# Two-layer gated cross-attention and MoE kernel: layer 0's row return and layer 1's preparation in one block, scales for eight tiles at once, rows normalised on ScalarE

## The chip, the cores and the metric

One core of one Trainium2 chip runs the kernel. The metric is the device time of one execution in microseconds (us). A difference of 0.2% is about what a measurement of this kernel can tell from none.

## What is computed

Two layers over x (2048 rows of 256, fp32). Each layer is a gated cross-attention and a gated mixture of experts, both on a layer norm without parameters. The context has 1601 rows of 192, 16 heads of 16.

```python
x = x + tanh(g_xattn[0]) * L0_xattn(_layernorm(x), ctx_768, ...)
x = x + tanh(g_ffn[0]) * L0_ffn(_layernorm(x), ...)      # shared expert + top 1 of 8
x = x + tanh(g_xattn[1]) * L1_xattn(_layernorm(x), ctx_768, ...)   # with an MLP behind it
x = x + tanh(g_ffn[1]) * L1_ffn(_layernorm(x), ...)      # top 2 of 8, norm with gamma, beta

def _layernorm(x, axis=-1, eps=1e-05):
    m = jnp.mean(x, axis=axis, keepdims=True)
    v = jnp.var(x, axis=axis, keepdims=True)
    return (x - m) / jnp.sqrt(v + eps)
```

In the attention, q is projected from the normed x, k and v from the context; the scores are exponentiated without subtracting a maximum, unless a bound on them is exceeded.

## The kernel before

x stays in SBUF as 16 tiles (128 rows by 256 columns each); four tiles make a block of 512 rows (TB is 4, NB is 4). `ps` is PSUM, 8 banks of 512 fp32. A layer runs as a sequence of `nc.Block`s; at the end of a block all engines meet. In a block each engine has its own list of instructions, in the order written, and waits on semaphores.

1. **Preparation** (L507). `transpose_block` (L634) turns four tiles of xn on TensorE into banks 0 and 1, ScalarE copies them (`turned`, L574), TensorE projects them with wq (`item`, eight matmuls, L652), ScalarE takes squares and the bf16 high part (L591, L592), VectorE splits off the middle and low parts (L736, L741, L743), SyncE stores the parts (L354). Layer 0 has four items of keys before the four of queries; layer 1 only those of queries, since its keys were made in layer 0. `norm` (L346) sums squares by head. At the end the largest norms give `unsafe` (L767 to L775). In layer 0 `norm_rows` makes xn here for eight tiles at once.
2. **The check block** (L798). If `unsafe` is set, all scores are scanned for maxima first; otherwise it is skipped.
3. **Attention** (L928). Four blocks of queries, each with 104 exponentials on ScalarE (L1182), fed by TensorE (L948, L964). Behind it come routing and loads; layer 0 also makes layer 1's keys here.
4. **Experts** (L1603). For each of 23 tiles (39 in layer 1) GpSimd fetches 128 rows (L1842), TensorE transposes (L1639) and multiplies (L1652, L1664), GpSimd scatters the result (L1855). In layer 0, TensorE and ScalarE then make layer 1's values (L375, L381). SyncE waits for the last scatter, reads the rows back in four pieces (L1612), spreads the ones row of the keys and loads layer 1's first keys (L361). VectorE, for each piece of four tiles, adds the rows to x (L1814) and calls `norm_rows`: statistics (L457), `norm_root` (L438 to L450, a chain in which each small instruction waits for the one before), and xn (L461).
5. `free_semaphores` (L290) clears the layer's semaphores, with a meeting of all engines.

Then layer 1's preparation starts; its first instructions on SyncE are seven loads of weights (w1, b1, w2, the two halves of b2, rw, rb; L544 to L553). `norm_scales` (L471) is used at the end of layer 1: it writes a scale and a shift for each row, and ScalarE (L1737) applies them.

Of the kernel before, what the change touches and what calls it, by code (L numbers as in the profile page):

```python
# [20 lines left out]
ALU = mybir.AluOpType  # L21
# [61 lines left out]
def build(nc, a, out):  # L83
    ctx = ExitStack()
    with ctx:
# [203 lines left out]

        def free_semaphores():  # L290
# [31 lines left out]
        s_wk, s_wv, s_wq, s_kin = ([keep(f"{w}_in{l}") for l in range(2)] for w in ("wk", "wv", "wq", "k2"))  # L322
# [89 lines left out]
        def consts_pool(pool):  # L412
# [20 lines left out]
                           allow_small_or_imprecise_dtypes=True)  # L433

# [39 lines left out]
        def layer(L):  # L474
            l = L.n
            NTL, T = L.tiles, L.slots

            s_w, s_xn, s_rs, s_m1p = sem(f"attn_weights{l}"), sem(f"xn{l}"), sem(f"rest{l}"), sem(f"mid_parts{l}")
            s_xt, s_xtc = sem(f"xn_transposed{l}"), sem(f"xnT_copied{l}")
            s_pr, s_hi, s_sp = sem(f"projected{l}"), sem(f"high_parts{l}"), sem(f"split{l}")  # L480
            s_po = [sem(f"parts_stored{l}_{i}") for i in range(PARTS)]
            s_v, s_va, s_vz = sem(f"v_projected{l}"), sem(f"v_copied{l}"), sem(f"v_padded{l}")
            s_sq, s_nrm = sem(f"squared{l}"), sem(f"norm_sums{l}")
            s_top, s_turn = sem(f"norm_top{l}"), sem(f"norm_turned{l}")
            s_k2, s_q2 = [sem(f"k2_in{l}_{g}") for g in range(NG)], [sem(f"q2_in{l}_{g}") for g in range(NG)]
            s_ctx = [sem(f"ctx_in{l}_{i}") for i in range(2)]
            s_rw = sem(f"router_in{l}")
# [19 lines left out]
            with nc.Block() as block:  # L507
                @block.sync
                def _(sp):
                    def store(n):  # L510
                        kind, b = items[n]
                        w = width(n)
                        sp.wait_ge(s_sp, n + 1)
                        store_parts(sp, (k_img if kind == "k" else q_img)[l],
                                    [part[n % PARTS][j][:, :, 0:w] for j in range(3)],
                                    slice(b * w, (b + 1) * w), kind == "q", s_po[n % PARTS])

                    if l == 0:
                        src = a["x"].rearrange("o (p t) d -> p (o t) d", p=P)

                        def load_x(b):
                            sp.dma_start(x[:, b * TB:(b + 1) * TB, :], src[:, b * TB:(b + 1) * TB, :]).then_inc(s_x[b], 16)

                        load_x(0)
                        load_x(1)
                        load_wk(sp, 0)
                        for i, cols in enumerate([slice(0, 2 * KB), slice(2 * KB, M)]):
                            for k in range(2):
                                sp.dma_start(ctxT[0:CH, k, cols], a["ctxT"][k * CH:(k + 1) * CH, cols]
                                             ).then_inc(s_ctx[i], 16)  # L530
                        load_wv(sp, 0)
                        load_x(2)
                        load_x(3)
                        load_wq(sp, 0)
                        for i, name in enumerate(["g_xattn", "g_ffn"]):
                            sp.dma_start(gates[:, 2 * i:2 * i + 2], spread(a[name], 2)).then_inc(s_gate, 16)
                        sp.wait_ge(s_zero, 1)
                        for i in range(2):
                            sp.dma_start(shift_dram[i].rearrange("r h s -> (r h) s").rearrange("a (n s) -> a n s", n=4),
                                         zero[0:SHIFT * H, 0:D].bitcast(BF16).unsqueeze(1)  # L540
                                         .broadcast_to([SHIFT * H, 4, 2 * D])).then_inc(s_sz, 16)
                        spread_ones(sp, s_k2[0])
                    if L.mlp:
                        sp.dma_start(w1[:, :, :], a["w1"].rearrange("(k p) n -> p k n", p=P)).then_inc(s_w, 16)  # L544
                        sp.dma_start(b1[:, :], a["b1"]).then_inc(s_w, 16)
                        sp.dma_start(w2[:, :, :], a["w2"].rearrange("(k p) n -> p k n", p=P)).then_inc(s_w, 16)
                    else:
                        sp.dma_start(w2[:, 0:KD, :], a["wo"].rearrange("(k p) n -> p k n", p=P)).then_inc(s_w, 16)
                    for i in range(2):
                        sp.dma_start(b2[:, i, :], spread(a[f"bo{l}"], D)).then_inc(s_w, 16)  # L550
                    sp.dma_start(rw[:, :, :], a[f"rw{l}"].rearrange("(k p) n -> p k n", p=P)).then_inc(s_rw, 16)
                    if l == 1:
                        sp.dma_start(rb[:, :], spread(a["rb1"], E)).then_inc(s_rw, 16)  # L553

                    for n in range(Q0):
                        store(n)
# [1356 lines left out]
```

## Time and profile before

| | |
|---|---|
| median of 3 runs | 1501.73 us (1501.42 to 1502.45) |
| the profiled execution | 1500.18 us, span 1498.4 us |
| TensorE busy | 1351.1 us, 90% |
| ScalarE busy | 975.1 us, 65% |
| VectorE busy | 549.3 us, 37% |
| GpSimd busy | 175.6 us, 12% |
| mean granted TensorE clock | 0.951 of full speed |

The profile names an instruction by line, engine, operation and tiles. PE is TensorE, ACT ScalarE, DVE VectorE, POOL GpSimd, SPq the queue of SyncE. The chain that ended last goes back through the expert loop of layer 1 (L1652 and L1664, 5% and 4% of the span) and doesn't reach the stretch between the layers; it has to be read by its timeline.

### The profile page before, as it was taken

What the parts mean: (1) busy time and instruction counts of PE and PEld (TensorE: products, weight loads), DVE (VectorE), ACT (ScalarE), POOL (GpSimd) and SP (SyncE); (2) the same over time, 40 slices, a digit from 0 to 9 for tenths busy, and PEclk for the clock granted to TensorE, in tenths of its full rate; (3) what the DMA queues carried; (4) which work ended last, traced back from release to release, by engine and by line L of the source; (5) the groups of instructions that cost most, each with busy time, mean ns of one, the idle gap of its engine ahead of it and who ended that gap; (6) DMA issues with size and microseconds to landing.
All of it is one profiled execution on the core that took longest, in us unless ns stands there. A gap on an engine that the chain in (4) does not pass through costs nothing. (4 is left out here: it accounts for less than half of the span.)

```text
span 1498.4 us, 31951 instructions
## 1 busy us (share of the span) xinstructions
PE 1351.1 (90%) x13236; PEld 716.5 (48%) x13236; DVE 549.3 (37%) x1242; ACT 975.1 (65%) x1162; POOL 175.6 (12%) x188
## 2 busy tenths in 40 slices
PE   7799999999999996999657999999999994399994
PEld 4433333333333654999533334334334333299983
DVE  7412152242423253443550222422422524544435
ACT  4499999999996323333137996995996990055532
POOL 2000000000001321333200000000000000166530
PEclk9899999999999997999878999999999997599997
DMA  7661010101011714111439110110111115012214
GB/s 209 157 119 27 20 26 20 27 20 26 23 33 60 247 56 142 40 47 47 109 93 179 26 27 15 34 27 16 33 27 46 65 33 166 18 58 75 72 59 166
DMA packets 65866, 100.82 MB, mean 67 GB/s; under 512 B 10074, under 2 KB 47966, under 8 KB 64952
## 3 DMA queue, kind: packets, MB, share of 16 engines
q1 hardware_dynamic: 59768, 82.47, 20.2%
q0 software_dynamic: 5952, 16.26, 3.3%
q8 instruction: 108, 1.77, 0.5%
q14 instruction: 38, 0.31, 0.1%
HBM read 67.99 MB, written 26.21 MB: 63 GB/s over the span
## 5 line engine op out<-in xcount | busy, mean ns | idle before, releaser
L1182 ACT ACTIVATE arena<-ps 128x1024 f32<-128x1024 f32 x556 | 553.9, 1219 | 57.2 <-PE ps L948 57.2
L948 PE MATMUL ps<-arena 99*32 99x512 bf16 x6656 | 465.9, 384 | 15.4 <-PEq L798 9.4
L948 PEld LDWEIGHTS ps<-arena 99*32 99x32 bf16 x6656 | 151.3, 95 | 405.8 <-issue 167.0
L1182 ACT ACTIVATE wqkv<-ps 128x1024 f32<-128x1024 f32 x276 | 294.3, 1221 | 22.7 <-PE ps L948 22.7
L964 PE MATMUL ps<-arena 128*32 128x512 f32 x2224 | 290.5, 594 | 1.0 <-ACT arena L1182 0.8
L1264 DVE COPY work<-ps 128x512 f32<-128x512 f32 x32 | 22.1, 692 | 405.4 <-PE ps L964 405.4
L1652 PEld LDWEIGHTS ps<-work,arena 128*128 128x128 f32 x1184 | 144.6, 195 | 6.5 <-DVE work L1745 3.5
L1652 PE MATMUL ps<-work,arena 128*128 128x128 f32 x1184 | 145.7, 279 | 2.1 <-DVE work L1745 2.1
L964 PE MATMUL ps<-wqkv,arena 128*32 128x512 f32 x1104 | 144.0, 593 | 0.0
L1842 POOL DMA_INDIRECT work<-xn_img,fetch x62 | 60.9, 983 | 628.7 <-POOLq L928 612.8
L1664 PE MATMUL ps<-arena,work 128*128 x496 | 117.2, 380 | 0.0
L1268 DVE RECIPROCAL work<-work 128x512 f32<-128x512 f32 x32 | 107.3, 3353 | 1.1
L964 PEld LDWEIGHTS ps<-arena 128*32 128x32 f32 x2224 | 68.8, 111 | 59.6 <-ACT arena L1182 2.6
L1664 PEld LDWEIGHTS ps<-arena,work 128*128 128x128 f32 x496 | 89.4, 190 | 10.1 <-issue 0.5
L1706 ACT ACTIVATE arena<-arena 128x1024 f32 x62 | 65.3, 1057 | 32.2 <-PEq L928 23.4
L1855 POOL DMA_INDIRECT y_tok<-work,dest x62 | 61.8, 996 | 141.4 <-DVE work L1780 81.3
L1579 POOL TENSOR_TENSOR arena<-arena 128x512 f32<-128x512 f32 x12 | 17.5, 1460 | 490.5 <-ACT arena L1202 490.5
L1723 ACT ACTIVATE work<-work 128x512 f32<-128x512 f32 x39 | 24.6, 630 | 74.2 <-DVE work L1760 74.2
L1717 ACT ACTIVATE work<-ps 128x512 f32<-128x512 f32 x23 | 13.7, 597 | 90.6 <-PE ps L1652 90.6
L1745 DVE COPY work<-ps 128x256 f32<-128x256 f32 x62 | 26.3, 425 | 119.1 <-PE ps L1639 119.1
L1290 DVE TENSOR_TENSOR work<-ps,b 128x512 f32<-128x512 f32 x16 | 11.1, 692 | 109.9 <-PE ps L989 104.6
L964 PEld LDWEIGHTS ps<-wqkv,arena 128*32 128x32 f32 x1104 | 34.2, 111 | 29.0 <-ACT wqkv L1182 0.7
(204 smaller groups left out, 1157.7 us busy)
## 6 DMA issues: line engine op xcount, KB each, us to landing
arena<-in_ew SPq DMA_DIRECT2D x16, 512.0 KB, 5.3
arena<-q_img SPq DMA_DIRECT2D x32, 192.0 KB
arena<-y_tok SPq DMA_DIRECT2D x12, 512.0 KB, 6.3
arena<-k_img SPq DMA_DIRECT2D x8, 624.0 KB, 12.9
q_img<-work SPq DMA_DIRECT2D x18, 256.0 KB, 2.6
k_img<-work SPq DMA_DIRECT2D x21, 208.0 KB, 2.5
arena<-q_img SPq DMA_DIRECT2D x32, 128.0 KB
work<-work SPq DMA_DIRECT2D x128, 32.0 KB, 2.0
```

Of the source, the lines that this page charges most:

```text
L948: last = nc.tensor.matmul(ps[i * VW:(i + 1) * VW, buf + j, :], k2[0:ROWS + SHIFT, h, at:at + VW], q2[0:ROWS + SHIFT, h, :], start=True, st ...
L964: last = nc.tensor.matmul(ps[j * VW:(j + 1) * VW, 6 + g % 2, :], v_aug[:, c, HG * g + j, :], probs[(b * STEPS + 2 * w + j // 2) % RING][:, ...
L1182: nc.scalar.activation(probs[(b * STEPS + u) % RING], ps[:, buf:buf + 2, :], ACT.Exp, scale=SCALE).then_inc(s_exp, 1)
L1264: nc.vector.tensor_copy(pv_sb, ps[:, 6 + g % 2, :]).then_inc(s_copy, 1)
L1268: nc.vector.reciprocal(sums, sums).then_inc(s_inv, 1)
L1652: last = nc.tensor.matmul(ps[:, 2 + 2 * (i % 2) + n, f * P:(f + 1) * P], w_now[i % 2][n][:, k, f * P:(f + 1) * P], rowsT[i % 2][:, k, :], ...
L1664: last = nc.tensor.matmul(ps[:, 6 + i % 2, 0:D], hT[i % 2][:, k, :], w_down[:, bass.ds(e, 1), k, :].rearrange("p a n -> p (a n)"), start=( ...
L1706: nc.scalar.activation(w_now[i % 2][0].rearrange("p k n -> p (k n)"), w_gate[l][:, bass.ds(e, 1), :, :].rearrange("p a k n -> p (a k n)"), ...
L1723: nc.scalar.activation(hT[i % 2], act_g[i % 2], ACT.Relu).then_inc(s_h, 1)
L1745: nc.vector.tensor_copy(rowsT[i % 2], ps[:, i % 2, 0:D].rearrange("p (k n) -> p k n", n=P)).then_inc(s_tc, 1)
L1842: nc.gpsimd.indirect_dma_start(out=rows_in[i % ROWBUFS], out_offset=None, in_=xn_img[l], in_offset=bass.IndirectOffsetOnAxis(ap=fetch[:, i ...
L1855: nc.gpsimd.indirect_dma_start(out=y_tok[l], out_offset=bass.IndirectOffsetOnAxis(ap=dest[:, i:i + 1], axis=0), in_=rows_out[i % 2], in_of ...
```

## The change

- The preparation becomes a function `prepare(l)` that returns the parts of each engine. Layer 0's stays a block of its own. Layer 1's is appended to layer 0's expert block, so that the engines don't meet between the row return and it. Its semaphores are kept over the end of the layer, and `free_semaphores` now runs behind it.
- Layer 1's seven loads of weights are issued by SyncE at the start of layer 0's expert block.
- VectorE adds two pieces of rows, takes statistics for eight tiles, and calls `norm_scales` once for the eight; this is done twice, for both halves.
- xn is written by ScalarE: eight activations (Identity with a scale and a bias for each row) for each half, the first half before `turned(0)`, the second behind item 0. TensorE's transposes of block b wait for 4(b + 1) of them.
- In layer 1's preparation TensorE does item 1 before the transposes of block 2, and blocks 2 and 3 before item 2.
- At layer 0's start the padding of the values shares the constants' counter on GpSimd. Semaphores that only one layer needs are made once.

```diff
@@ layer 0's expert block
                 @block.sync
                 def _(sp):
                     if l == 0:
+                        preps[1][0](sp)
                         sp.wait_ge(s_dn, NTL)
...
                     if l == 0:
-                        spread_ones(sp, s_kin[1], 2)
+                        spread_ones(sp, s_kin, 2)
                         for i in range(2):
                             sp.wait_ge(s_kd[i], 96)
-                        load_k2(sp, 1, 0, s_kin[1])
+                        load_k2(sp, 1, 0, s_kin)
+                        preps[1][1](sp)
...
                             project_v(c, c % 4).then_inc(s_v, 1)
+                        pe.wait_ge(s_va, NC)
+                        pe.wait_ge(s_y, NTL)
+                        preps[1][3](pe)
...
                             copy_v(c, c % 4).then_inc(s_va, 1)
+                        preps[1][2](act)
...
                     if l == 0:
-                        for b in range(NB):
-                            ts = slice(b * TB, (b + 1) * TB)
-                            dve.wait_ge(s_back[b], 16)
-                            chain(nc.vector.scalar_tensor_tensor(
-                                out=x[:, ts, :].rearrange("p t d -> p (t d)"),
-                                in0=got[0][:, ts, :].rearrange("p t d -> p (t d)"), scalar=tg,
-                                in1=x[:, ts, :].rearrange("p t d -> p (t d)"), op0=ALU.mult, op1=ALU.add))
-                            chain(norm_rows(chain, lambda t: x[:, b * TB + t, :], lambda t: xn[:, b * TB + t, :]))
+                        n = 2 * TB
+                        for i in range(2):
+                            for b in range(2 * i, 2 * i + 2):
+                                ts = slice(b * TB, (b + 1) * TB)
+                                dve.wait_ge(s_back[b], 16)
+                                last = nc.vector.scalar_tensor_tensor(
+                                    out=x[:, ts, :].rearrange("p t d -> p (t d)"),
+                                    in0=got[0][:, ts, :].rearrange("p t d -> p (t d)"), scalar=tg,
+                                    in1=x[:, ts, :].rearrange("p t d -> p (t d)"), op0=ALU.mult, op1=ALU.add)
+                            chain(last)
+                            for t in range(n):
+                                last = nc.vector.bn_stats(stats[:, t, :], x[:, i * n + t, :])
+                            norm_scales(chain, last, n, scales[:, 0, i * n:(i + 1) * n],
+                                        scales[:, 1, i * n:(i + 1) * n]).then_inc(s_lnx, 1)
+                        preps[1][4](dve, chain)
@@ prepare(l), layer 1's parts
+                def normed(i):
+                    act.wait_ge(s_lnx, i + 1)
+                    for t in range(i * 2 * TB, (i + 1) * 2 * TB):
+                        nc.scalar.activation(xn[:, t, :], x[:, t, :], ACT.Identity, bias=scales[:, 1, t:t + 1],
+                                             scale=scales[:, 0, t:t + 1]).then_inc(s_nx, 1)
...
+                else:
+                    normed(0)
+                    turned(0)
+                    turned(1)
+                    act.wait_ge(s_wq[l], 48)
+                    item(0)
+                    normed(1)
+                    turned(2)
+                    item(1)
+                    turned(3)
+                    item(2)
+                    item(3)
...
+                def transpose_block(b):
                     if l == 0:
+                        pe.wait_ge(s_xn, b // 2 + 1)
+                    else:
+                        pe.wait_ge(s_nx, TB * (b + 1))
...
+                else:
+                    transpose_block(0)
+                    transpose_block(1)
+                    pe.wait_ge(s_wq[1], 48)
+                    item(0)
+                    item(1)
+                    norm(0)
+                    transpose_block(2)
+                    transpose_block(3)
+                    item(2)
+                    norm(1)
+                    item(3)
+                    norm(2)
+                    norm(3)
@@ consts and padding
-                        consts_pool(pool)
-                        pad_v(Chain(pool, "v_pad_chain"))
+                    pad_v(consts_pool(pool))
```

## Rows read from the trace of the kernel before

**Rows 1.** Windows: stretch, length, busy us (instructions) per engine, clock, DMA share, GB/s.
```profile
735.00:759.00 24.00, 0.00 (x0) 0.00 (x0) 21.89 (x96) 0.33 (x1) 0.00 (x0) 0.55 0.41 66
```
**Rows 2.** Timeline, VectorE, layer 0's row return: start, us, instruction, count [idle before].
```profile
732.19 1.28 DVE L1814 SCALAR_TENSOR_TENSOR x<-arena,tgate,x 128x1024 f32<-128x1024 f32 x1 [8.09 <-DMA arena<-y_tok]
...
733.51 1.40 DVE L457 BATCH_NORM_STATS2 stats<-x 128x6 f32<-128x256 f32 x4
...
737.82 1.38 DVE L461 TENSOR_SCALAR xn<-x,mv,root_bits 128x256 f32<-128x256 f32 x4
...
758.94 1.38 DVE L461 TENSOR_SCALAR xn<-x,mv,root_bits 128x256 f32<-128x256 f32 x4
```
**Rows 3.** Timeline, layer 1's preparation from its first transpose to the flag.
```profile
762.11 1.94 PE L634 MATMUL ps<-ident,xn 128*128 128x128 f32 x8 [27.20 <-PEq L293]
...
767.17 1.02 ACT L574 ACTIVATE arena<-ps 128x1024 f32<-128x1024 f32 x1 [2.06 <-PE ps L634]
...
771.72 0.68 ACT L592 ACTIVATE work<-ps,bq 128x512 bf16<-128x512 f32 x1
...
784.50 0.68 ACT L592 ACTIVATE work<-ps,bq 128x512 bf16<-128x512 f32 x1
...
785.29 1.41 DVE L736 SCALAR_TENSOR_TENSOR work<-ps,bq,work 128x512 f32<-128x512 f32 x2
...
791.08 0.14 DVE L775 TENSOR_SCALAR unsafe<-tops 1x1 int32<-1x1 f32 x1
```
**Rows 4.** Timeline, flag and first exponential: layer 0's two, then layer 1's exponential.
```profile
61.75 0.14 DVE L775 TENSOR_SCALAR unsafe<-tops 1x1 int32<-1x1 f32 x1
...
68.63 3.77 ACT L1182 ACTIVATE arena<-ps 128x1024 f32<-128x1024 f32 x4 [7.82 <-PE ps L948]
...
797.11 3.77 ACT L1182 ACTIVATE arena<-ps 128x1024 f32<-128x1024 f32 x4 [2.61 <-PE ps L948]
```
**Rows 5.** DMA issues of the second and fourth row read (us to landing); window, TensorE only.
```profile
arena<-y_tok SPq DMA_DIRECT2D x1, 512.0 KB, 4.8
...
arena<-y_tok SPq DMA_DIRECT2D x1, 512.0 KB, 8.7
...
730.00:735.00 5.00, 4.91 (x23) 1.00 0.98 368
```
**Rows 6.** Timeline, layer 0's preparation: statistics and xn of its second eight tiles.
```profile
31.24 2.71 DVE L457 BATCH_NORM_STATS2 stats<-x 128x6 f32<-128x256 f32 x8
...
37.16 2.67 DVE L461 TENSOR_SCALAR xn<-x,mv,root_bits 128x256 f32<-128x256 f32 x8
```
**Rows 7.** Timeline, end of layer 1: scales written by VectorE, applied by ScalarE.
```profile
1477.42 0.17 DVE L470 COPY scales<-root_bits 128x8 f32<-128x8 f32 x1
...
1477.70 3.76 ACT L1737 ACTIVATE arena<-ps,scales 128x256 f32<-128x256 f32 x8 [24.86 <-DVE scales L471]
```
**Rows 8.** Page, part 5: groups of ScalarE from SBUF and from PSUM (mean ns).
```profile
L1723 ACT ACTIVATE work<-work 128x512 f32<-128x512 f32 x39 | 24.6, 630 | 74.2 <-DVE work L1760 74.2
L1717 ACT ACTIVATE work<-ps 128x512 f32<-128x512 f32 x23 | 13.7, 597 | 90.6 <-PE ps L1652 90.6
```
**Rows 9.** Timeline, start of layer 0's expert loop; DMA issues, w1 and w2.
```profile
590.34 1.14 POOL L1842 DMA_INDIRECT work<-xn_img,fetch  x1 [43.80 <-POOLq L928]
...
593.25 0.69 PE L1639 MATMUL ps<-ident,work 128*128 128x128 f32 x2 [8.02 <-DMA work<-xn_img,fetch]
...
w<-in_w SPq DMA_DIRECT2D x2, 512.0 KB, 4.0
```
**Rows 10.** Window (TensorE only: busy, clock, DMA, GB/s); timeline, layer 0's query items.
```profile
768.00:770.00 2.00, 2.00 (x5) 0.98 0.38 74
...
42.03 4.37 PE L652 MATMUL ps<-arena,wqkv 128*128 128x512 f32 x7
...
47.40 7.11 PE L652 MATMUL ps<-arena,wqkv 128*128 128x512 f32 x16
```
**Rows 11.** Timeline, the maximum of the head norms on VectorE.
```profile
788.72 0.42 DVE L767 TENSOR_REDUCE norms<-ps 128x4 f32<-128x256 f32 x1
```

More of the change, by code:

```diff
@@ L288, in sem, with only @@
             return sems[name]
+        def only(needed, name):
+            return sem(name) if needed else None
         def free_semaphores():
@@ new lines, in sync, with store @@
+            def sync(sp):
+                def store(n):
+                    kind, b = items[n]
+                    w = width(n)
+                    sp.wait_ge(s_sp, n + 1)
+                    store_parts(sp, (k_img if kind == "k" else q_img)[l],
+                                [part[n % PARTS][j][:, :, 0:w] for j in range(3)],
+                                slice(b * w, (b + 1) * w), kind == "q", s_po[n % PARTS])
+                for n in range(Q0):
+                    store(n)
+                if l == 0:
+                    for i in range(PARTS):
+                        sp.wait_ge(s_po[i], stored(i, Q0))
+                    load_k2(sp, 0, 0, s_k2[0])
+                    sp.wait_ge(s_sz, 32)
+                store(Q0)
+                store(Q0 + 1)
+                sp.wait_ge(s_po[Q0 % PARTS], stored(Q0 % PARTS, Q0 + 1))
+                load_q2(sp, 0, 0)
+                store(Q0 + 2)
+                store(Q0 + 3)
+                sp.wait_ge(s_w, 16 * (5 if mlp else 3))
@@ new lines, in scalar, with tensor, item @@
+                if l == 0:
+                    values(range(7, NC))
+                    act.wait_ge(s_gate, 32)
+                    nc.scalar.activation(tgate[:, :], gates[:, :], ACT.Tanh)
+            def tensor(pe):
+                def transpose_block(b):
+                    if l == 0:
+                        pe.wait_ge(s_xn, b // 2 + 1)
+                    else:
+                        pe.wait_ge(s_nx, TB * (b + 1))
+                    if b:
+                        pe.wait_ge(s_xtc, b)
+                    for t in range(TB):
+                        for k in range(KD):
+                            last = nc.tensor.transpose(ps[:, k, t * P:(t + 1) * P],
+                                                       xn[:, b * TB + t, k * P:(k + 1) * P], ident[:, :])
+                    last.then_inc(s_xt, 1)
+                def item(n):
+                    kind, b = items[n]
+                    if kind == "k":
+                        pe.wait_ge(s_ctx[b // 2], 32)
+                    else:
+                        pe.wait_ge(s_xtc, b + 1)
+                    if n >= 2:
+                        pe.wait_ge(s_rs, n - 1)
+                    for ko in range(KD):
+                        bank = 4 + 2 * (n % 2) + ko
@@ L777, in _ @@
[L777 to L782 removed]
+                    pe.wait_ge(s_xtc, NB)
+                    values(range(7, 9))
+                    norm(Q0 + 3)
+                    values(range(9, NC))
+                else:
+                    transpose_block(0)
+                    transpose_block(1)
+                    pe.wait_ge(s_wq[1], 48)
+                    item(0)
+                    item(1)
+                    norm(0)
+                    transpose_block(2)
+                    transpose_block(3)
+                    item(2)
+                    norm(1)
+                    item(3)
+                    norm(2)
+                    norm(3)
```

468 lines of the change are left out of this document (206 added, 262 removed).

## The prediction

> **What bounds the kernel now.** I read the page first: TensorE is busy 90% of the span, and its slices drop to nothing in two places only, the hand-over from layer 0 to layer 1 and the end. The change works in the first of these, so I read that stretch by itself. The table by windows says what kind of stretch it is: from 735 to 759 us TensorE has no instruction and ScalarE one, while VectorE is busy 21.9 of 24 us and nothing else competes [rows 1]. The timeline of VectorE shows why [rows 2]: the rows of the first block land, VectorE adds them to x at 732.19, takes statistics, takes the root in a chain of dependent small instructions, and normalises four tiles; four times over, the last tile being done at 758.94 + 1.38 = 760.32. Only then does the block end. TensorE's first transpose of the preparation starts at 762.11, having sat idle 27.20 us, although its first tiles had long been ready [rows 3]. From there the preparation is a chain through TensorE, ScalarE and VectorE that ends with the safety flag at 791.08 + 0.14 = 791.22 [rows 3], and the first exponential of layer 1 starts at 797.11 [rows 4]. Before this stretch (the expert loop) and behind it (attention) the order of the work is unchanged, so a microsecond won here is a microsecond won at the end, as long as neither neighbour is disturbed.
>
> **The change part by part, first what comes before the first transpose.** The clock of this path starts at 732.19, when the first block of rows is in; the change leaves that alone [rows 2].
> Two additions of rows instead of one: 1.28 us each. The second one's rows were issued at 728.67 (one issue of 0.43 us behind the first) and took 4.8 us, so they are there at 733.5, the very moment VectorE wants them; the last block took 8.7 us and is there at 738.3, before the second half asks at 741 [rows 5]. So statistics start at 732.19 + 2 x 1.28 = 734.8.
> Statistics and root for eight tiles: layer 0's preparation does the same for eight, 37.16 - 31.24 = 5.92 us [rows 6]. For four it took 737.82 - 733.51 = 4.31 [rows 2]: the small instructions cost the same for eight columns as for four, and that is where two of four root chains are saved. 740.7.
> The two small instructions that write scale and shift, and the hand-over to ScalarE: 1477.70 - 1477.42 = 0.28 [rows 7]. ScalarE starts at 741.0.
> Normalising on ScalarE: the end of the kernel has the same instruction on the same shape, from PSUM, eight in 3.76 us [rows 7]. Here the source is SBUF; the pair of ScalarE groups on 128x512 puts SBUF at 630 ns against 597 [rows 8], so 0.03 more each. Four tiles take about 2.0, all eight 3.9. The first transpose waits for four: 741.0 + 2.0 + 0.1 = 743.1. It now starts at 762.11, so this part gives 19.0 us. ScalarE is free for it: its last value copy ends near 735.3, and what is queued behind the wait for the scales is only this preparation.
> The Trainium skill (ScalarE: Activation LUTs, "What ACT_TABLE_LOAD costs") speaks against putting this work on ScalarE: each [128,1] pointer operand adds about 93 ns, and an ACTIVATE with none takes 186 ns + 0.833 ns an element. An estimate from that page is 585 ns a tile and 0.49 us from start to start, against VectorE's 0.35 for the same tile [rows 2]; by it the sum would be about 0.3 us worse.
>
> **Then what comes behind the first transpose.** In the kernel before, transpose to last flag takes 791.22 - 762.11 = 29.1 us [rows 3]. I redo it with the new order. Up to the end of ScalarE's work on item 0 nothing differs (both transposes start on a cold TensorE, with the same waits): 771.72 + 0.68 - 762.11 = 10.3 after the first transpose [rows 3], so 753.4. Now ScalarE normalises the second eight tiles; their scales were ready long before (VectorE: 741 + 2.6 + 5.9 + 0.3 = 749.7). 753.4 + 3.9 = 757.3. TensorE meanwhile does item 1 and transposes block 2 once its four tiles are there, so ScalarE goes on at once: copy of block 2 (1.02 [rows 3]) to 758.3, item 1 (four activations, 2.45) to 760.7, copy of block 3 to 761.8. Items 2 and 3 are then bound by TensorE (3.6 to 3.7 us for eight matmuls, by the sixteen in 7.11 [rows 10], from 759.4): ScalarE ends near 768.4. That is 15.0 after item 0, against 784.50 + 0.68 - 772.40 = 12.8 before [rows 3]: of the 3.9 that ScalarE got extra, some 1.7 hides behind the reordered item 1. VectorE needs 791.22 - 785.29 = 5.9 from its last item to the flag [rows 3]: 774.35. The preparation ends 791.22 - 774.35 = 16.9 us sooner.
> The stores of the parts and the load of the first queries, on SyncE's queue, follow VectorE's items and move with them. Before them on that queue stand now the four row reads, the ones and the first keys, all issued by 732.3; a store is wanted at 757 at the earliest. Nothing.
>
> **What is moved elsewhere.** The block's end with the freeing of semaphores now stands between the flag and attention instead of before the transposes. Nothing in the trace shows this sum. The place before costs 762.11 - 760.32 = 1.8 us with freeing; from flag to first exponential it is 5.9 in layer 1, and 68.63 - 61.89 = 6.7 in layer 0, both without [rows 3, 4]. I take +0.5 for the freeing, between -0.5 (it hides behind the wait for instructions) and +2.
> The seven weight loads of layer 1 leave the preparation, where nothing waited for them. They go to the start of layer 0's expert loop, 1.3 MB in front of nothing on SyncE but beside GpSimd's first row fetch, whose landing starts the loop: issued 590.34, transposed 593.25, with TensorE 8.02 idle for it [rows 9]. A 512 KB load lands in 4.0 [rows 9], so its packets move just when the fetch's do. Everything behind the fetch is TensorE-bound, so the delay goes through whole. Bounds: 0, and 3.5 us (1.3 MB at the 368 GB/s that the row reads reached [rows 5]). I take +0.7, near the low end: a fetch of 128 KB shares the engines with one load only.
> Startup: the padding of the values uses another counter on GpSimd, in the shade of the loads. Nothing.
>
> **Sum.** -16.9 + 0.5 + 0.7 = -15.7 us. The profiled execution took 1500.18 (span 1498.4), so it would become 1484.5; the median of the three runs is 1501.73, 1.55 above it, so the forecast is 1486.0. Its own range is 1483 to 1489.5: -0.5 and 0 for the two moved costs at one end, +2 and +2.5 at the other.
>
> **Rivals.** (a) The moved costs bite: the loads delay not one fetch but the whole start of the loop (3.5), and the wait for instructions behind the flag grows to the 2 to 3 us by which the two layers' starts may differ. 1501.7 - 16.9 + 3.5 + 3 = 1491. For it: no cover for either. Against: both are short, once each. (b) TensorE's clock stays low. The granted clock averages 0.55 of full speed over the idle stretch [rows 1], so nearly all of it at 1.2 GHz, and is back only 6 us into the preparation (0.98 from 768 to 770) [rows 10]. In layer 0 seven matmuls of an item took 4.37 us after a gap, where sixteen later took 7.11 [rows 10]. The new order gives TensorE smaller portions with waits for ScalarE between. At 1.2 GHz throughout, each item takes 7.4 instead of 3.7 us and each transpose group 0.9 more; walking the same chain, the flag comes about 17 us later than at 774.35, and all is given back: 1503. Against it: those sixteen in layer 0 follow right behind the slow seven and one group of transposes, so the clock came back within one item although the gaps there are of the same size. The Trainium skill (TensorE: Matmul & The Clock Gate, "HAM oscillation — how this bites in real kernels") describes this giving back, bursts with waits between that all start cold. (c) Slower than before: the safety branch. The new form x * scale + shift rounds otherwise than (x - mean) * root, and the product of the largest norms is compared with 1600 / 0.0625 = 25600. If it passes that point, attention first scans all scores: 16 heads x 16 tiles of VectorE reductions over 1604 columns; with 0.42 us for 256 columns [rows 11] that is some 1.8 us each, 470 us, so about 1955. Nothing in the trace says how near the product is, only that the branch isn't taken in either layer; a rounding change decides it only at the edge. (d) The change does more than I count: the instruction wait of the removed block boundary was part of the 5.9 us behind the flag, and the loads cost nothing. 1481.
>
> **How the numbers follow.** Forecast 0.79, (a) 0.10, (b) 0.05, (c) 0.01, (d) 0.05. The time is the forecast's, 1486.0. The range from 1482.5 to 1491 takes in the forecast's own and most of (a) and (d). A measurement of this kernel can tell about 0.2%, 3 us, from no change. Faster by more: the forecast, (a), (d), and a partial form of (b), 0.95; within: (b), 0.04; slower: (c), 0.01.
>
> **What would show it.** First transpose of the second preparation 11 us after the first addition of rows, not 30; ScalarE's eight activations in about 3.9 us, twice; flag some 42 us after that first addition instead of 59; first exponential 6 to 7 us behind the flag; the first expert tile's transpose within 1 us of where it was. The prediction is wrong if the granted clock is at half in the items, if ScalarE normalises its second half before item 0 or waits for its scales, if the first fetch of the expert loop takes over 4 us, or if attention runs at another pace.

## The result and the profile after

The changed kernel takes 1488.26 us (median of 4, 1488.12 to 1489.22) against 1502.09 (1501.42 to 1502.86): ratio 0.9906, interval 0.9892 to 0.9920. Forecast were 1486.0 and a range from 1482.5 to 1491. The profiled executions have spans of 1498.4 and 1486.5 us.

The timeline of the changed stretch, line by line against [rows 2, 3, 4, 7]; L1872 is the old L1814, L657 the old L634, L584 ScalarE's new rows, L607 the old L592, L804 the flag, L998 and L1232 attention's first matmuls and exponentials. Columns: start, us, instruction, count, idle before.

```profile
734.96 2.58 DVE L1872 SCALAR_TENSOR_TENSOR x<-arena,tgate,x 128x1024 f32<-128x1024 f32 x2 [7.80 <-DMA arena<-y_tok]
...
743.76 4.04 ACT L584 ACTIVATE xn<-x,scales 128x256 f32<-128x256 f32 x8 [5.38 <-DVE scales L477]
745.98 1.94 PE L657 MATMUL ps<-ident,xn 128*128 128x128 f32 x8 [8.02 <-ACT xn L584]
...
756.92 0.68 ACT L607 ACTIVATE work<-ps,bq 128x512 bf16<-128x512 f32 x1
757.49 4.03 ACT L584 ACTIVATE xn<-x,scales 128x256 f32<-128x256 f32 x8
...
772.20 1.41 DVE L765 SCALAR_TENSOR_TENSOR work<-ps,bq,work 128x512 f32<-128x512 f32 x2 [0.32 <-ACT work L607]
...
777.98 0.14 DVE L804 TENSOR_SCALAR unsafe<-tops 1x1 int32<-1x1 f32 x1
...
781.61 1.01 PE L998 MATMUL ps<-arena 99*32 99x512 bf16 x5 [4.30 <-PEq L848]
...
784.58 4.55 PE L998 MATMUL ps<-arena 99*32 99x512 bf16 x43 [1.96 <-issue]
...
785.24 3.77 ACT L1232 ACTIVATE arena<-ps 128x1024 f32<-128x1024 f32 x4 [2.54 <-PE ps L998]
```

TensorE waits 8.02 us for its first rows, not 27.20, and the flag is there at 778.12. The start of layer 0's expert loop in the same timeline, against [rows 9]:

```profile
590.96 1.14 POOL L1905 DMA_INDIRECT work<-xn_img,fetch  x1 [43.90 <-POOLq L978]
...
595.86 0.69 PE L1691 MATMUL ps<-ident,work 128*128 128x128 f32 x2 [10.33 <-DMA work<-xn_img,fetch]
```

The DMA issue of that fetch, in the list of DMA issues (the last number is us from issue to landing):

```profile
work<-xn_img,fetch POOLq DMA_INDIRECT x1, 4.9
```

From these marks, stage by stage, in us:

| stage | before | after | difference | forecast |
|---|---|---|---|---|
| start to issue of the first row fetch | 590.34 | 590.96 | +0.6 | 0 |
| first row fetch to its transpose | 2.91 | 4.90 | +2.0 | +0.7 |
| from there to the first addition of rows | 138.94 | 139.10 | +0.2 | 0 |
| first addition to first transpose | 29.92 | 11.02 | -18.9 | -19.0 |
| first transpose to flag | 29.11 | 32.14 | +3.0 | +2.1 |
| flag to first exponential | 5.89 | 7.12 | +1.2 | +0.5 |
| from there to the end | 701.29 | 701.26 | 0.0 | 0 |
| sum | 1498.4 | 1486.5 | -11.9 | -15.7 |

By the traces the change gives 11.9 us, by the medians 13.8. The stages hold for one execution each; how far they repeat is the last experiment.

### The profile page after: what moved, and what is told of

Read it like the earlier page. It is cut to its first block and busy times, and to the rows that moved or that the text cites. A ratio compares the mean times of both kernels' runs of the same rounds, so it can differ in the third digit from the quotient of the medians.

```text
span 1486.5 us, 31922 instructions
## 1 busy us (share of the span) xinstructions
PE 1352.8 (91%) x13236; PEld 715.3 (48%) x13236; DVE 539.6 (36%) x1204; ACT 982.6 (66%) x1178; POOL 175.0 (12%) x188
## 5 line engine op out<-in xcount | busy, mean ns | idle before, releaser
L1232 ACT ACTIVATE arena<-ps 128x1024 f32<-128x1024 f32 x556 | 554.5, 1224 | 56.7 <-PE ps L998 56.7
L998 PE MATMUL ps<-arena 99*32 99x512 bf16 x6656 | 465.5, 384 | 16.8 <-PEq L848 10.9
L998 PEld LDWEIGHTS ps<-arena 99*32 99x32 bf16 x6656 | 149.8, 95 | 408.5 <-issue 168.2
L1232 ACT ACTIVATE wqkv<-ps 128x1024 f32<-128x1024 f32 x276 | 294.9, 1225 | 22.7 <-PE ps L998 22.7
```

The costliest lines, as they stand in the source:

```text
L998: last = nc.tensor.matmul(ps[i * VW:(i + 1) * VW, buf + j, :], k2[0:ROWS + SHIFT, h, at:at + VW], q2[0:ROWS + SHIFT, h, :], start=True, st ...
L1232: nc.scalar.activation(probs[(b * STEPS + u) % RING], ps[:, buf:buf + 2, :], ACT.Exp, scale=SCALE).then_inc(s_exp, 1)
```

## The experiments

"Flag at" is always the time behind the first addition of rows: 59.03 in the kernel before, 43.16 in the changed one. The runs were measured in three groups, each beside the kernel before. Its medians there were 1501.75 (loads_late, fused_only, batched_only, vector_rows), 1500.37 (warm_pe, second_meeting, late_vector, late_vector_warm) and 1502.35 (before_early, warm_pe_short, late_vector_short, after_again).

### The loads behind the first keys (loads_late)

```diff
@@ layer 0's expert block, SyncE
-                        preps[1][0](sp)
                         sp.wait_ge(s_dn, NTL)
...
                         load_k2(sp, 1, 0, s_kin)
+                        preps[1][0](sp)
                         preps[1][1](sp)
```

> The changed kernel with one thing undone: SyncE issues layer 1's seven weight loads behind the row reads and the first keys, not at the start of layer 0's expert loop. Theory: the loads delay the first row fetch of the loop, which landed 4.9 us after its issue against 2.8; with them gone the first transpose of the loop comes 2.9 us after the fetch's issue again, and the time falls by 2.0 to 2.5 us, to about 1486.0. In their new place they run behind the first keys and ahead of the first store, so the flag stays 43.2 us behind the first addition of rows. Rival one: the late start of the loop is the code's place or the clock, and nothing changes (1488.3). Rival two: the loads now push the stores of the parts and the first queries; the flag or the first exponential comes up to 3 us later and the gain is lost (1488 to 1489).

Measured: 1484.22 us (1483.81 to 1485.45), ratio 0.9889 (0.9873 to 0.9906). The loop's start and SyncE's queue:

```profile
589.08 1.14 POOL L1905 DMA_INDIRECT work<-xn_img,fetch  x1 [43.86 <-POOLq L978]
...
592.11 0.69 PE L1691 MATMUL ps<-ident,work 128*128 128x128 f32 x2 [8.13 <-DMA work<-xn_img,fetch]
...
731.28 0.42 SPq L544 DMA_DIRECT2D w<-in_w  x1
...
742.86 0.47 SPq L553 DMA_DIRECT2D rb<-in_rb  x1
...
756.74 8.63 SPq L359 DMA_DIRECT2D q_img<-work  x6
```

The fetch lands in 3.03 again. In their new place the loads are issued by 743.3, and the first store is wanted at 756.7: flag at 42.75, flag to exponential 7.12, nothing given back. Both rivals fall. The time fell by 4.0, though (4.6 by the spans). The fetch explains 1.9, the loop behind it 0.2, and the preparation, where the clock came up 0.7 sooner, 0.4. Another 1.9 stands ahead of the fetch's issue (589.08 against 590.96), where the code is the same.

### The loads alone, in the kernel before (before_early)

```diff
@@ layer 0's expert block, SyncE, in the kernel before; the same loads are taken out of layer 1's preparation
                     if l == 0:
+                        sp.dma_start(w1[:, :, :], a["w1"].rearrange("(k p) n -> p k n", p=P)).then_inc(s_w1, 16)
...
+                        sp.dma_start(rb[:, :], spread(a["rb1"], E)).then_inc(s_rw1, 16)
                         sp.wait_ge(s_dn, NTL)
```

> The kernel before with one part of the change alone: layer 1's seven weight loads issued at the start of layer 0's expert loop instead of at the start of layer 1's preparation. Theory: the first row fetch of the loop lands 4.9 to 5.8 us after its issue (2.9 before), the rest is as before, flag 59.0 behind the first addition: 2 to 3 us slower than the kernel before, about 1503. Rival: the preparation gets back what the loop loses (its first transposes and copies no longer share SBUF with 1.3 MB of loads), within 0.5 us of before.

Measured: 1504.30 us against 1502.35, ratio 1.0015 (1.0003 to 1.0026).

```profile
590.70 1.14 POOL L1852 DMA_INDIRECT work<-xn_img,fetch  x1 [43.85 <-POOLq L931]
...
596.37 0.69 PE L1649 MATMUL ps<-ident,work 128*128 128x128 f32 x2 [11.09 <-DMA work<-xn_img,fetch]
```

5.67 us from issue to transpose instead of 2.91, flag at 59.11. So this part of the change costs 2.8 us by the traces and 2.0 by the medians (0.5 to 3.9 by the interval), and the preparation gives nothing back.

### The merging without the rest (fused_only)

```diff
@@ VectorE, layer 0's row return, in the changed kernel; normed() is taken out of ScalarE's list
-                            norm_scales(chain, last, n, scales[:, 0, i * n:(i + 1) * n],
-                                        scales[:, 1, i * n:(i + 1) * n]).then_inc(s_lnx, 1)
+                            norm_rows(chain, lambda t: x[:, b * TB + t, :], lambda t: xn[:, b * TB + t, :]
+                                      ).then_inc(s_nx, TB)
```

> The changed kernel with the merged block and the new order kept, but VectorE works as before the change: four times additions, statistics, root and rows of xn for four tiles each, and the transposes of a block wait only for its own four tiles; ScalarE normalises nothing. Theory: the merging carries nearly all of the gain. First transpose 7 us behind the first addition of rows, flag about 45 us behind it (43.2 in the changed kernel, 59.0 before): time about 1490. Rival: the scales for eight at once and ScalarE's rows carry it, the merging only the meeting of the engines (1.8 us): flag about 52 to 57, time 1497 to 1502.

Measured: 1491.35 us (1490.84 to 1492.07), ratio 0.9935 (0.9919 to 0.9952).

```profile
734.72 1.28 DVE L1869 SCALAR_TENSOR_TENSOR x<-arena,tgate,x 128x1024 f32<-128x1024 f32 x1 [8.04 <-DMA arena<-y_tok]
...
741.87 1.94 PE L655 MATMUL ps<-ident,xn 128*128 128x128 f32 x8 [4.38 <-DVE xn L467]
...
761.45 1.38 DVE L467 TENSOR_SCALAR xn<-x,mv,root_bits 128x256 f32<-128x256 f32 x4
...
764.42 5.06 PE L673 MATMUL ps<-arena,wqkv 128*128 128x512 f32 x8 [0.41 <-DVE work L763]
...
780.38 0.14 DVE L802 TENSOR_SCALAR unsafe<-tops 1x1 int32<-1x1 f32 x1
```

The first transpose comes at 7.15, earlier than in the changed kernel; the last rows come at 28.1 and then hold the end. Flag at 45.80: the merging, with the new order of items and transposes, moves the flag by 13.2 of the 15.9 us. The order by itself wasn't run. The rival (52 to 57) falls. Some 1.5 us are lost here to TensorE's clock: it is at half again from 763.8 to 767.2, behind a wait of 2.7 us for VectorE's last rows, and item 2 takes 5.06 us where it takes 3.60 in the changed kernel.

### Scales for eight and ScalarE's rows without the merging (batched_only)

```diff
@@ the kernel before: VectorE's loop as in the change; ScalarE, behind the value copies, in the same block
+                        for i in range(2):
+                            act.wait_ge(s_lnx, i + 1)
+                            for t in range(i * 2 * TB, (i + 1) * 2 * TB):
+                                nc.scalar.activation(xn[:, t, :], x[:, t, :], ACT.Identity, bias=scales[:, 1, t:t + 1],
+                                                     scale=scales[:, 0, t:t + 1])
```

> The kernel before, with only the other half of the change: VectorE makes scales for eight tiles at once, twice, and ScalarE writes the rows of xn, both still in a block that ends before the preparation. Theory: ScalarE ends its 16 rows 21.6 us after the first addition of rows (VectorE needed 28.1), so the first transpose comes 6.5 us sooner, the preparation itself takes its 29.1 us, and the time falls by 6.5 to about 1495.6. The two halves of the change then overlap: each alone is worth much more than what it adds to the other (about 2 for this one). Rival: the parts simply add, and this one is worth the 15.9 less what the merging gives, 2 us: 1500.

Measured: 1494.17 us (1492.47 to 1495.44), ratio 0.9949 (0.9932 to 0.9965).

```profile
732.74 2.59 DVE L1823 SCALAR_TENSOR_TENSOR x<-arena,tgate,x 128x1024 f32<-128x1024 f32 x2 [7.95 <-DMA arena<-y_tok]
...
755.72 1.94 PE L636 MATMUL ps<-ident,xn 128*128 128x128 f32 x8 [20.13 <-PEq L293]
...
785.48 0.14 DVE L777 TENSOR_SCALAR unsafe<-tops 1x1 int32<-1x1 f32 x1
```

First transpose at 22.98, flag at 52.88: 6.2 us sooner than before, near the expected 6.5. The halves overlap: 13.2 and 6.2 alone, 15.9 together. Once the blocks are merged, the other half is worth 2.6, with the 1.5 of the clock in it.

### Who writes the rows (vector_rows)

```diff
@@ VectorE, in the changed kernel; normed() is taken out of ScalarE's list
+                            norm_root(chain, n)
+                            for t in range(n):
+                                nc.vector.tensor_scalar(xn[:, i * n + t, :], x[:, i * n + t, :], mv[:, t, 0:1],
+                                                        rstd[:, t:t + 1], ALU.subtract, ALU.mult).then_inc(s_nx, 1)
```

> The changed kernel, but VectorE writes the rows of xn itself (eight tiles at once, one semaphore count for each), and ScalarE normalises nothing. Theory: in the preparation ScalarE stands on the path and VectorE has room, so ScalarE's second eight rows cost more than they save: first transpose 10 us behind the first addition (11.0 in the changed kernel), VectorE done with both halves at 22.4, flag at 41.5 to 42.5 instead of 43.2, time 1487 to 1488. Rival: taking the rows off VectorE is what pays; VectorE is then the bound, the flag comes at 46 or later and the time is 1491.

Measured: 1486.72 us (1486.63 to 1486.97), ratio 0.9903 (0.9886 to 0.9919).

```profile
745.88 1.94 PE L655 MATMUL ps<-ident,xn 128*128 128x128 f32 x8 [7.16 <-DVE xn L1881]
...
755.49 2.67 DVE L1881 TENSOR_SCALAR xn<-x,mv,root_bits 128x256 f32<-128x256 f32 x8
...
761.28 1.07 PE L655 MATMUL ps<-ident,xn 128*128 128x128 f32 x8 [1.20 <-ACT arena L589]
...
776.70 0.14 DVE L802 TENSOR_SCALAR unsafe<-tops 1x1 int32<-1x1 f32 x1
```

The line at 761.28 is the transposes of block 3. In the changed kernel the transposes of blocks 2 and 3 read

```profile
759.77 1.07 PE L657 MATMUL ps<-ident,xn 128*128 128x128 f32 x8
762.57 1.07 PE L657 MATMUL ps<-ident,xn 128*128 128x128 f32 x8 [1.73 <-ACT arena L589]
```

Flag at 41.03. So of the second half of the change, the statistics and roots for eight at once give 4.8 us (45.80 to 41.03, again with the 1.5 of the clock in it), and with the rows on ScalarE 2.1 are lost again (to 43.16). The timelines split these 2.1. The first transpose comes 1.0 later (11.02 against 10.07). Block 2's transposes wait for no rows in either kernel, since TensorE is still at item 1; but block 2's copy stands behind ScalarE's second eight rows (4.03 us), so block 3's transposes wait 1.73 instead of 1.20 us: 0.5. The other 0.7 lie before the end of item 0 (11.62 against 10.95 behind the first transpose), where the two differ only in when the clock rose. Without them the rows on ScalarE cost 1.5. The pair with late loads (loads_late and late_vector, below) gives the same: flag 42.75 against 41.83, and item 0 ends at 11.26 against 11.82. VectorE had room for the rows: in the changed kernel it waits 5.3 us for item 0. By time the difference is 1.3 to 1.5, which the intervals alone wouldn't tell apart.

### TensorE's clock (warm_pe, warm_pe_short)

In the changed kernel's preparation the clock (columns: window, length, TensorE busy with its count, granted clock, DMA share, GB/s) came up late:

```profile
751.00:752.00 1.00, 1.00 (x3) 0.50 0.00 0
...
753.00:754.00 1.00, 1.00 (x2) 0.50 0.00 0
754.00:755.00 1.00, 1.00 (x3) 0.73 0.00 0
755.00:756.00 1.00, 1.00 (x4) 1.00 0.00 0
```

Half the clock (1.2 GHz) until 754.5, 8.5 us behind the first transpose, where the kernel before had it back after 6 [rows 10]. Neither is a constant: the other two kernels that aren't merged had it back after 6.1 (before_early) and 7.5 (batched_only), and the six traces with merged blocks, eight tiles at once and no matmuls added after 7.2 to 9.0.

```diff
@@ TensorE, layer 0's expert block, in the changed kernel (56 in warm_pe, 30 in warm_pe_short)
                         pe.wait_ge(s_y, NTL)
+                        for _ in range(56):
+                            nc.tensor.matmul(ps[:, 7, 0:P], ident[:, :], ident[:, :], start=True, stop=True)
                         preps[1][3](pe)
```

> The changed kernel with 56 more matmuls of the identity by itself (128x128, bank 7, read by nobody) between layer 1's values and the first transpose; they fill the 8 us in which TensorE waits for ScalarE's first rows. Theory: the granted clock then is 1.0 instead of 0.5 through both first transposes and item 0, which ends 8.5 to 9 us behind the first transpose instead of 11.6 (10.3 in the kernel before); the flag comes 2.5 to 3.2 us sooner, 40 to 40.7 behind the first addition of rows, and the time falls to about 1485.3. Rival: VectorE and ScalarE, not TensorE, set this stretch (ScalarE's second eight rows stand behind item 0 in any case), and the flag moves by less than 1 us.

Measured: 1488.52 us (1485.05 to 1492.17), ratio 0.9908 (0.9887 to 0.9929). My count was wrong:

```profile
739.82 12.77 PE L1738 MATMUL ps<-ident 128*128 128x128 f32 x112 [0.47 <-ACT arena L386]
...
752.43 1.04 PE L657 MATMUL ps<-ident,xn 128*128 128x128 f32 x8
```

56 written fp32 matmuls are 112 instructions, and the first transpose waits until 16.01. Behind it item 0 ends after 8.04 us instead of 11.62, and the flag comes after 28.57 instead of 32.14. So with half as many:

> The changed kernel with 30 unused matmuls of the identity ahead of the first transpose, not 56. A written fp32 matmul of 128 columns turned out to be two instructions, so the 56 took 12.8 us and held the first transpose back by 5 us; behind that transpose everything was faster (item 0 ended 8.0 us behind it, not 11.6; the flag came 28.6 behind it, not 32.1). Theory: 30 take 6.9 us and end before the first rows are there, so the first transpose comes 11.0 behind the first addition of rows as before and the flag at 39.6 instead of 43.2. Time 3.5 us under the changed kernel run beside it. Rival: with a gap of some tenths of a microsecond only, the matmuls and ScalarE's or VectorE's reads disturb each other or the clock falls once more; flag at 42 to 43.

Measured: 1483.23 us (1482.61 to 1484.41), ratio 0.9875 (0.9858 to 0.9892), against 1488.05 for the changed kernel beside it.

```profile
744.62 1.09 PE L657 MATMUL ps<-ident,xn 128*128 128x128 f32 x8 [0.81 <-ACT xn L584]
...
747.58 1.06 PE L657 MATMUL ps<-ident,xn 128*128 128x128 f32 x8 [1.87 <-ACT arena L589]
...
773.76 0.14 DVE L804 TENSOR_SCALAR unsafe<-tops 1x1 int32<-1x1 f32 x1
...
777.42 5.31 PE L998 MATMUL ps<-arena 99*32 99x512 bf16 x48 [4.32 <-PEq L848]
```

The clock, in windows with the columns as above:

```profile
736.00:744.00 8.00, 7.33 (x62) 1.00 1.10 189
744.00:756.00 12.00, 9.51 (x44) 1.00 0.07 18
```

First transpose at 10.93, flag at 40.21, 2.9 us sooner than in the changed kernel beside it (43.13). The cold clock is thus worth 2.9 us on the path, not the 3.5 I expected: the second transposes now wait for ScalarE, which still normalises. The rest of the gain wasn't expected: flag to first exponential falls to 4.62, because the pause ("issue", 1.65 us in the changed kernel beside it, 1.96 in the first) inside attention's first matmuls is gone.

### The freeing of the semaphores (second_meeting)

```diff
             free_semaphores()
+            if L.n == 0:
+                nc.all_engine_barrier()
```

> The changed kernel with one more meeting of all engines behind the freeing of layer 0's semaphores. From flag to first exponential the changed kernel takes 7.12 us, the kernel before 5.89: the freeing with its meeting now stands on the path. Theory: a meeting costs what the engines' exchange costs, 0.4 to 0.8 us, and that comes on top: 7.5 to 7.9 from flag to first exponential. Rival: what the 7.12 shows is a wait for instructions behind the block's end, and one more meeting hides in it: 7.1 still.

Measured, one execution: 1483.43 us, flag at 42.98, flag to first exponential 7.45.

```profile
780.04 0.62 PE L998 MATMUL ps<-arena 99*32 99x512 bf16 x4 [4.62 <-PEq L848]
...
783.00 4.31 PE L998 MATMUL ps<-arena 99*32 99x512 bf16 x44 [2.34 <-issue]
```

From the flag to attention's first matmul it takes 2.1 to 2.3 us in the three kernels that aren't merged, 3.5 to 3.6 in the ten other merged traces, and 3.8 here. So the freeing costs about 1.3 us on the path, and one more meeting 0.3, a little less than I thought. The pause hides none of it and is itself still there. Flag to first exponential, which holds the pause too, is 5.89, 5.74 and 5.45 in the three kernels that aren't merged, and 6.8 to 7.4 in the six traces with merged blocks, no matmuls added and no second meeting. Leaving out the freeing wasn't tried. The single time says nothing against the changed kernel; see the last experiment.

### Putting parts together (late_vector, late_vector_warm, late_vector_short)

> Two undone parts together: the loads behind the first keys, and xn written by VectorE, eight rows at once, ScalarE normalising nothing. Theory: the two lie in different stretches and add: loop's first fetch lands in 2.9 to 3.0 us, flag 41.0 behind the first addition, time 1484.2 - 2.1 = about 1482. Rival: the loads now meet VectorE's earlier items and their stores; the flag or the first exponential gives back 1 to 2 us: 1484.

Measured: 1483.39 us (1483.07 to 1485.02), ratio 0.9881 (0.9864 to 0.9898). Fetch in 2.95, flag at 41.83: 0.8 later than with VectorE's rows alone, and the time lies between the theory (1482) and the rival (1484). TensorE's cold part was 0.9 longer in this execution (item 0 ended 11.8 behind the first transpose, there 10.95). So nothing says that the loads met VectorE's items. By the ratio it can't be told from loads_late.

> The kernel with late loads and VectorE's rows, with 48 unused matmuls ahead of the first transpose. Theory: with TensorE at the full clock, items 0 and 1 are done before VectorE has the second eight rows, so VectorE is what block 2 waits for: block 2's transposes start 21 to 21.3 us behind the first addition (23.2 without), flag at 39 instead of 41, time about 1480. Rival: no gain, the clock falls again in the waits between the items.

Measured: 1482.85 us (1482.07 to 1485.71), ratio 0.9876 (0.9859 to 0.9894). The same miscount as in warm_pe: first transpose at 14.01, flag at 42.06, so it doesn't test its theory. Flag to first exponential is 4.60, again without the pause.

> Late loads, xn written by VectorE, and 27 unused matmuls ahead of the first transpose. Theory: first transpose at 10.0 behind the first addition, items 0 and 1 done by 20, so that block 2 waits only for VectorE's rows (21.1): flag at 39.3 instead of 41.0 to 41.8. The fastest of all, about 1481 if the start and end of the kernel are as in the runs before. Rival: as VectorE is the bound for block 2, TensorE's clock gives at most 1 us: flag at 40.5.

Measured: 1482.88 us (1482.01 to 1483.81), ratio 0.9870 (0.9854 to 0.9887).

```profile
753.32 1.09 PE L655 MATMUL ps<-ident,xn 128*128 128x128 f32 x8 [0.72 <-DVE xn L1883]
...
757.04 4.76 PE L673 MATMUL ps<-arena,wqkv 128*128 128x512 f32 x8
```

And TensorE's clock there, in windows with the columns as above:

```profile
752.00:760.00 8.00, 6.08 (x30) 0.79 0.15 47
```

Flag at 40.61, where the theory had 39.3 and the rival 40.5. Item 0 ends at 18.05, as it should, and block 2 starts at 21.1 on VectorE's last rows. But the clock falls once more behind the waits around block 2 (0.79 from 752 to 760), and item 2 takes 4.76 us instead of 3.6: what comes earlier is partly paid back in clock. The four fastest (late_vector_warm, this one, warm_pe_short, late_vector: 1482.85 to 1483.39) can't be told apart by their intervals. Each of their executions is faster than all eight of the changed kernel (1485.71 at most against 1486.36 at least). The best pair by the stages, late loads with warm_pe_short, wasn't run.

### How far it repeats (after_again)

> The changed kernel itself once more, beside the three others. Theory: what differs between executions of one kernel lies outside the changed stretch, at the start (the flag of layer 0 came between 60.8 and 64.8 us in the runs so far) and in the last 40 us (39.6 to 42.6, by when TensorE's clock rises); the stretch itself repeats: first row fetch lands after 4.9 to 5.8, first transpose 11.0 and flag 42.7 to 43.2 behind the first addition, 7.1 from flag to first exponential. Rival: the changed stretch varies by a microsecond or more too, and the differences of 1 to 2 us read so far from single traces are not safe.

Measured: 1488.05 us (1486.36 to 1488.76), ratio 0.9904 (0.9886 to 0.9921). Fetch 5.24, first transpose 11.00, flag at 43.13, flag to exponential 6.81. The stretch repeats within 0.1 us in these two, what lies around it within 0.5 (the loop from its first transpose to the first addition 139.10 and 139.57). With the same code in the stretch, loads_late and second_meeting have the flag at 42.75 and 42.98, so single traces are good to about 0.4 there. Further out the executions differ more: layer 0's flag came between 60.8 and 64.8 us, and from the last scatter to the end it took 39.7 (second_meeting) to 42.6 us (changed kernel), 41.1 in the kernel before. The clock at that place in the kernel before:

```profile
1466.00:1468.00 2.00, 2.00 (x6) 0.55 1.02 414
```

In the changed kernel:

```profile
1455.00:1457.00 2.00, 2.00 (x6) 0.50 1.02 406
```

And in second_meeting:

```profile
1449.00:1451.00 2.00, 1.26 (x6) 1.00 1.01 393
```

There the clock comes up 3 us, 6 us and 0 us behind the first of 64 matmuls. That is 3 us of time between programs whose code there is the same.

## Why the prediction held, and where its terms were off

The sum had every stage, and the range held the time. That the forecast itself came within 2.3 us is in part luck, as said below. The largest term was right to 0.1 us: first addition to first transpose 18.9 against 19.0, with its parts (statistics and root for eight 5.9, hand-over, four rows) as read from [rows 6, 7]. Its smallest part was off: eight rows on ScalarE take 4.04, not the 3.9 I made of [rows 7, 8]. The estimate from the Trainium skill (ScalarE: Activation LUTs, "What ACT_TABLE_LOAD costs"), 585 ns and 0.49 us from start to start, gives 4.03, and the trace agrees with it to 0.01. That they are dearer there than on VectorE shows in the flag too: 1.5 to 2.1 us (vector_rows).

The sum was 3.8 us too good by the traces. Four terms were too small, 3.9 us together:

- **"I take +0.7, near the low end: a fetch of 128 KB shares the engines with one load only."** This was the largest miss. It costs 2.0 in the changed kernel's trace and 2.2 to 2.9 in the seven others with early loads (fetch to transpose 5.1 to 5.85, against 2.9 to 3.0). The step assumed that only w1 is in flight by then. In the trace w2's load is issued at 591.18, 0.2 us behind the fetch, takes 4.7 us and lands together with it. Two kernels show it from both sides, loads_late and before_early. Rival (a) had this mechanism with 3.5. By the prediction's own signs this step is refuted: the first fetch takes over 4 us, and the loop's first transpose comes 2.6 us later, not within 1.
- **"Up to the end of ScalarE's work on item 0 nothing differs (both transposes start on a cold TensorE, with the same waits)": 10.3.** It was 11.6. The waits were nearly the same (1.11 and 1.21 us ahead of the second transposes), the moment at which the clock rises was not: 6 us behind the first transpose before, 8.5 after. Part of this is chance, since kernels that aren't merged had 6.0 to 7.5. That is rival (b) in small. By warm_pe_short the whole cold part is worth 2.9 us, where the sum had it as a constant of the old trace. The Trainium skill's picture of bursts that all start cold (TensorE: Matmul & The Clock Gate, "HAM oscillation — how this bites in real kernels") isn't what happened: the clock stayed up from 755 to 775, over a wait of 1.7 us. Two runs do show a second fall inside the preparation, fused_only and late_vector_short.
- **"I take +0.5 for the freeing."** 1.2 here, 1.3 from the flag to attention's first matmul over the traces. I had bounded it by the old block boundary as a whole; at the new place nothing covers it.
- **Start of the kernel**: 0.6, by chance; in after_again the fetch is issued 0.7 earlier than in the kernel before.

The loop gave another 0.2 and the stretch before the first transpose 0.1, while what follows item 0 was reckoned 0.4 too long: ScalarE ends 14.5 us behind it, not 15.0. Two slips didn't enter the sum. The lower end of the forecast's own range, 1483, doesn't follow from its terms, which give 1484.3. And TensorE's slices on the page don't drop to nothing: the lowest are 5 tenths at the hand-over and 3 at the end; it is the table by windows that shows the empty stretch.

The medians hide part of this: their difference is 13.8, not 11.9. The forecast carried over the 1.55 by which the profiled execution of before lay under its median; the profiled execution of after lies 0.06 above its own. With the trace's -11.9 it would have said 1489.8. So the forecast is 2.3 off, not 3.8, by luck, through an offset that isn't understood: the kernel before ranged from 1497.8 to 1505.4 in thirteen runs of the last group. Likewise open is why loads_late gained 4.0 by time with 2.4 in its stages from the fetch's issue to the first exponential.

Of rival (a) the delay of the loads came, with 2.0 instead of 3.5, and the growing wait for instructions didn't. Rival (c), the safety branch, didn't come: the first exponential follows the flag within 7.5 us in each trace. Rival (d) didn't either: both moved costs were real.

What the change does, in one line: merging the blocks, with the new order, 13.2 of 15.9 us at the flag; statistics and roots for eight at once 4.8 more (1.5 of it clock); rows on ScalarE take 2.1 of that back (0.7 of it clock); the loads moved ahead cost 2.0 to 2.9, the freeing moved onto the path 1.2.

## What to carry to other kernels

Where one engine prepares data in pieces and a meeting of all engines stands between it and the consumers, the meeting's cost is not its own microsecond or two but the overlap that it forbids; remove it before tuning the pieces. Before work is moved to a less busy engine, ask what waits for that engine in that very stretch: ScalarE was idle over the stretch and still on the path. A load with no deadline shouldn't be issued where a stage starts on a fetch; put it where its queue has time, as it had here behind the first keys.

## What the runs showed of the hardware

- The granted clock of TensorE rises at different distances from the first matmul for the same code: 6.0 to 7.5 us in the preparation of the kernels that aren't merged, 7.2 to 9.0 in the merged ones with eight tiles at once, 0 to 6 us at the end of the kernel, where the 64 matmuls take 14.05, 15.54 and 17.07 us accordingly. One trace's cold stretch is no constant; a microsecond or two of a comparison of single executions can be this, three at the end of the kernel.
- Unused matmuls in an 8 us wait held the clock at full (1.00 from 736 to 756 in warm_pe_short, where it was at half from 741 to 754.5 in the changed kernel), and that was worth 2.9 us of path.
- TensorE paused for 1.5 to 2.3 us inside attention's first group, after 4 to 6 matmuls, in the kernel before too. In the four kernels with unused matmuls (54 to 112 instructions more on TensorE) the pause is gone and flag to first exponential is 4.6. It looks like the fetching of instructions: the pause comes after 6 matmuls in the kernels that aren't merged, after 5 in the merged ones, and after 4 with the second meeting's code ahead. The Trainium skill (Runtime: NRT & Kernel Launch, "Instruction fetch mechanics") says that a branch past the pages at hand has to fetch its target first. But in all fourteen traces one packet of an instruction queue moves within 1 us of attention's first matmul, with the pause and without, so the packet doesn't tell them apart. No run changed the amount of code alone, so this is argued, not shown.
